# Bf16 products with unread results, placed in four waits of TensorE

## The reference, cut to what matters

```python
h = _L0_tok_ref(x, ...)
h = h + _L0_attn_ref(_layernorm(h, axis=-1), ...)
h = h + _L0_ffn_ref(_layernorm(h, axis=-1), ...)
h = h + _L1_attn_ref(_layernorm(h, axis=-1), ...)
h = h + _L1_ffn_ref(_layernorm(h, axis=-1), ...)

# _L0_tok_ref, for each of 4 layers:
x = _layernorm(x + o, g1[i], be1[i])                      # o: attention output
f = jax.nn.relu(x @ W1[i] + b1[i]) @ W2[i] + b2[i]
x = _layernorm(x + f, g2[i], be2[i])
# then a last _layernorm(x, gf, bf)

# _L0_attn_ref:
qkv = xn @ w_qkv                                          # xn: normalised input
q_l = q.reshape(B, HEADS, M, l, DIM_HEAD).sum(3) / l      # landmarks; k_l likewise
sim1, sim2, sim3 = q @ k_l.T, q_l @ k_l.T, q_l @ k.T      # each through a softmax: a1, a2, a3
left = a1 @ moore_penrose(a2)                             # 6 iterations
out = left @ (a3 @ v) + conv(v)
```

## Time and profile before

| | |
|---|---|
| runs | 1103.89, 1107.82, 1109.42 us; median 1107.82 |
| profiled execution, its own time | 1105.52 us |
| its span | 1103.7 us, 21069 instructions |
| TensorE busy | 974.3 us, 88% |
| VectorE, ScalarE, GpSimd busy | 608.5 (55%), 592.2 (54%), 428.5 us (39%) |
| mean granted clock of TensorE | 0.928 |

### The profile page before, as it was taken

The page is one execution under the profiler, slowest core; times in us unless marked ns, Lnnn a source line. Parts: engine busy times, 40 slices in busy tenths (PEclk is TensorE's granted clock), DMA queues, the critical chain, the costliest instruction groups (busy, mean ns, idle before and its releaser), DMA issues. The chain is left out here.

```text
span 1103.7 us, 21069 instructions
## 1 busy us (share of the span) xinstructions
PE 974.3 (88%) x7350; PEld 711.0 (64%) x7350; DVE 608.5 (55%) x1802; ACT 592.2 (54%) x1332; POOL 428.5 (39%) x630
## 2 busy tenths in 40 slices
PE   2399999999999998626898999996899999997898
PEld 1256676667666665413776776784688888885564
DVE  4366776666667675136353111125377767784773
ACT  4166676676667665326435444316455555543476
POOL 6426777776667766648103000014400010037200
PEclk9699999999999999866698899998799999996899
DMA  4855444555464440010100111100000010006841
GB/s 126 176 106 133 94 94 100 141 117 111 102 154 95 94 94 12 1 33 0 47 3 10 29 30 29 46 8 1 20 10 11 11 56 14 1 1 148 207 97 37
DMA packets 54416, 71.82 MB, mean 65 GB/s; under 512 B 9476, under 2 KB 46624, under 8 KB 50464
## 3 DMA queue, kind: packets, MB, share of 16 engines
q1 hardware_dynamic: 53160, 67.33, 26.2%
q0 software_dynamic: 1152, 3.15, 1.1%
HBM read 48.96 MB, written 17.56 MB: 60 GB/s over the span
## 5 line engine op out<-in xcount | busy, mean ns | idle before, releaser
L2237 DVE TENSOR_REDUCE t_nmax<-banks 128x2 f32<-128x512 f32 x256 | 166.5, 685 | 84.5 <-PE banks L2047 79.3
L2166 ACT ACTIVATE t_probs<-banks 128x512 f32<-128x512 f32 x256 | 144.8, 592 | 79.8 <-PE banks L2069 78.4
L2047 PE MATMUL banks<-t_packed 96*128 96x256 bf16 x512 | 91.2, 278 | 15.3 <-DMA t_packed<-t_qk_pairs 13.3
L2325 POOL TENSOR_SCALAR xhat<-t_rbuf,mv,rstd 128x128 f32<-128x128 f32 x128 | 100.1, 795 | 3.3
L2069 PE MATMUL banks<-t_packed 120*128 120x256 bf16 x512 | 91.5, 276 | 9.3 <-DMA t_packed<-t_mT 8.7
L2047 PEld LDWEIGHTS banks<-t_packed 96*128 96x128 bf16 x512 | 47.5, 99 | 55.0 <-issue 27.0
L863 ACT ACTIVATE hid<-banks,b 128x512 f32<-128x512 f32 x64 | 43.5, 686 | 70.7 <-PE banks L768 70.0
L2069 PEld LDWEIGHTS banks<-t_packed 120*128 120x128 bf16 x512 | 46.3, 98 | 47.5 <-issue 21.0
L1197 ACT ACTIVATE l_probs<-banks,l_shift 128x256 f32<-128x256 f32 x128 | 59.4, 472 | 28.2 <-DVE l_shift L1238 25.5
L906 DVE SCALAR_TENSOR_TENSOR acc<-banks,gates,acc 128x128 f32<-128x128 f32 (+1 forms) x72 | 20.1, 342 | 98.0 <-PE banks L788 98.0
L2082 PE MATMUL banks<-t_probs,t_v 128*32 128x256 f32 x1024 | 72.3, 387 | 0.6 <-ACT t_probs L2166 0.6
(11 more groups left out here) (378 smaller groups left out, 2101.2 us busy)
## 6 DMA issues: line engine op xcount, KB each, us to landing
t_qk_pairs<-t_parts SPq DMA_DIRECT2D x32, 384.0 KB, 2.5
t_packed<-t_qk_pairs SPq DMA_DIRECT2D x32, 384.0 KB, 5.4
t_packed<-t_qk_pairs SPq DMA_DIRECT2D x32, 256.0 KB, 6.0
t_packed<-t_qk_pairs SPq DMA_DIRECT2D x32, 128.0 KB, 6.7
w<-in_L_ffn_w SPq DMA_DIRECT2D x16, 256.0 KB, 2.7
t_packed<-t_mT SPq DMA_DIRECT2D x32, 96.0 KB
g_qk_pairs<-g_parts SPq DMA_DIRECT2D x8, 384.0 KB, 5.3
g_packed<-g_qk_pairs SPq DMA_DIRECT2D x8, 384.0 KB, 4.7
```

The source lines that it names most:

```text
L2047: ins = pe.matmul(m.mbank[:, n % 3, i * S:(i + 1) * S], m.packed[0:MROW, 0, p, h, c + qt * P:c + (qt + 1) * P], m.packed[0:MROW, 1, p, h, ...
L2166: act.activation(m.probs[:, n % 6, :], m.sbank[:, n % 2, :], ACT.Exp).then_inc(sem["probs_ready"], 1)
L2237: dve.tensor_reduce(m.nmax[:, b, u // 4, 2 * hp:2 * hp + 2], m.mbank[:, n % 3, :].rearrange("p (i k) -> p i k", i=2), AX.X, ALU.max, negat ...
L2325: ins = pool.tensor_scalar(m.xhat[:, k, i, :], m.rbuf[:, k, i, :], m.mv[:, k, i, 0:1], m.rstd[:, k, i:i + 1], ALU.subtract, ALU.mult)
```

## The change

A helper issues `count` products of the bf16 identity (128x128) with itself repeated to 512 columns, into a bank that nobody reads at that time. It is called ahead of three items of the mixer, with bank 7, and ahead of C2 of the last pair, with the first bank of `m.mbank`; that one first waits until all maxima are taken. Each call stands ahead of the wait of the item that it precedes.

```diff
--- before.py
+++ after.py
@@ -74,6 +74,12 @@
 MTILES = B + 1
 
 
+def keep_clock(pe, m, bank, count):
+
+    for _ in range(count):
+        pe.matmul(bank, m.identb[:, :], m.identb[:, :].unsqueeze(1).broadcast_to([P, 4, P]), start=True, stop=True)
+
+
 def mixer_order():
 
     order = [("F", 0), ("F", 1), ("F", 2), ("VT",), ("H", 0), ("F", 3), ("VO",), ("H", 1), ("N", 0), ("NT", 0), ("H", 2), ("N", 1),
@@ -94,6 +100,7 @@
     return order
 
 
+CLOCK_PASSES = {("NT", 0): 14, ("NT", 2): 4, ("QK", 2): 5}
 INVERSE = ("SC", "A", "B", "Z")
 
 
@@ -206,6 +213,7 @@
 
             for item in order:
                 kind, g = item[0], item[-1]
+                keep_clock(pe, m, banks[:, 7, :], CLOCK_PASSES.get(item, 0))
                 if kind == "VT":
                     bank = use(("VO",))
                     pe.wait_ge(sem["mix_w_loaded"], 32)
@@ -2111,6 +2119,9 @@
                 filled(step, g, ins)
             elif step in ("C2", "C5"):
                 norm = "C1" if step == "C2" else "C4"
+                if (step, g) == ("C2", LAYER_PAIRS - 1):
+                    pe.wait_ge(sem["max_taken"], 16 * LAYER_PAIRS)
+                    keep_clock(pe, m, m.mbank[:, 0, :], 20)
                 pe.wait_ge(sem["xhat_ready"], apply_at[(norm, g)] + 1)
                 bank = use(step, g)
                 for i in range(4):
```

## The result

The changed kernel takes 1104.18 us (median of 20 runs, 1098.98 to 1110.98), the kernel before 1109.69 us (20 runs, 1103.88 to 1117.08). The ratio is 0.9953, 95% interval [0.9932, 0.9974]: 5.2 us faster, between 2.9 and 7.5.

What follows compares the result with a forecast made beforehand. Bound: a few TensorE waits at the last pair and mixer front, and the half clock behind them. 1.1 + 1.9 = 3.0 us off 1105.52 gives 1102.5; the runs' median lies 2.3 above the profiled execution: 1104.8 us, range 1100.0 to 1109.8.

Steps and rivals of the forecast that it cites:

- Passes at 0.22 us, hidden: Ahead of the last pair's C2: 20 passes at full clock take 4.4 us, inside TensorE's wait of 6.8 us.
- The pair, 1.1 us of 2.2: Last pair, C2's start to C4's: 2.2 us gained if the clock stays full, 0 if not; half taken, 1.1 us.
- The rows on idleness: Trace waits at full clock: 1.7 us passed unharmed; the 2.4 us left at the pair nearer to those losing the clock.
- The front part, 1.9 us: Mixer's front part: passes ahead of NT 0, NT 2 and QK 2 gain 1.9 us, bounds -3 and 2.6.
- QK 3's own 0.9 us: Mixer's front part: QK 3 takes 1.03 us at full clock in place of 1.91 at half, another 0.9 us.
- TensorE as the bound from 517.9 to 541.6: Behind the front part: TensorE, busy 21.9 of 23.7 us at half clock, hands the front part's gain on.
- rival 2: Clock holds on into the stretch of mostly 16-row products from 517.9, saving 3 us more: 1100.0 us; chance 0.08.
- The rule of the Trainium skill on transposes: Transposes don't count as TensorE work for the clock; by it the front part gains nothing and the sum is 1.1 us.
- That the passes don't act on the clock (3): At the pair and NT 0: identity passes, nearly all zeros, leave the clock unchanged, no gain: 1107.8 us; chance 0.12.
- That the nine are met by half clock (5): Passes ahead of NT 2 and QK 2 run at half clock, 3.2 us lost: about 1110.8 us; chance 0.09.
- That the clock holds at both places (1): Clock stays full through last pair and front part, 2.2 + 2.6 = 4.8 us gained: 1103.0 us; chance 0.20.

Runs made afterwards that it cites:

- e5: The changed kernel with no passes at all, only the added wait on max_taken left; ratio to the kernel before 1.0001 [0.9980, 1.0021].
- e1: The changed kernel with only the 20 passes ahead of the last pair's C2, none in the front part; ratio to the kernel before 0.9964 [0.9934, 0.9995].
- e4: The changed kernel with only the 4 passes ahead of NT 2 and 5 ahead of QK 2; ratio to the kernel before 1.0017 [0.9993, 1.0042].
- e3: The kernel before plus the wait and 31 passes ahead of the last pair's C2, none in the front part; ratio to the kernel before 0.9955 [0.9924, 0.9985].
- e2: The changed kernel with only the front part's 14, 4 and 5 passes, none at the pair; ratio to the kernel before 0.9957 [0.9933, 0.9982].
- e7: The changed kernel with 31 passes at the pair, not 20, and 24 more between the 16-row products; ratio to the kernel before 0.9954 [0.9931, 0.9977].
- e9: The changed kernel measured again without an edit, in a second group of runs; ratio to the kernel before 0.9955 [0.9927, 0.9983].
- e6: The changed kernel with 31 passes in place of 20 ahead of the last pair's C2; ratio to the kernel before 0.9951 [0.9923, 0.9979].

## Why the prediction was right, point by point

**The time.** Forecast 1104.8 us; measured 1104.18, in the range. The gain forecast was 3.0 us and the measured one 5.2 [2.9, 7.5]. That the two times agree within 0.6 us is luck: the kernel before came out at 1109.69 in 20 runs, not 1107.82 as in three, 1.9 us higher, and the gain was forecast 2.2 us too small. The two nearly cancel.

**Passes at 0.22 us, hidden.** Right. Twenty took 4.48 us (0.22 each), the four and five at full clock 1.04 and 1.25. All 31 fit into the wait. The added wait costs nothing (e5).

**The pair, 1.1 us of 2.2.** The mechanism was right and so was the bound (6.25 us; 6.3 had been read off the pair before). The term of the sum was too large by the profiled executions: the pair took 8.46 us on the mean of three with 20 passes and 8.90 on the mean of five without (8.51, 8.76, 8.84, 9.16, 9.25), 0.45 us, and since the two sets overlap even that is not clear of their scatter. One of the three is the slowest execution of e1, so the mean over all executions may be more; it is not known. The rows on idleness had said that 2.4 us is among the lengths that lose the clock, and half the gain was taken nevertheless. A fall that comes later puts C2 at full clock but keeps C3 at half longer (e1).

**The front part, 1.9 us.** Right in its steps as far as QK 3. NT 0 was not late, the hand-overs went as ScalarE's steps said (N 2 1.94 us earlier, forecast 2.0), and q 2 waited 0.24 us (0.3). QK 3's own 0.9 us was a property of the execution shown: four other executions without the 14 passes had it at 1.03. From NT 0's start to QK 3's end it is 14.25 us in five executions with all three groups of passes against 15.74 on the mean of five without the 14, 1.5 us.

Behind QK 3 the step that failed is what hands the gain on. The prediction had TensorE as the bound from 517.9 to 541.6, with nothing gained there. But in the same trace TensorE waits in that stretch for VectorE's a2 (1.35 us, to 528.75), and a2 of the second pair stands beside GpSimd's memsets:

```profile
522.40 1.80 POOL L602 MEMSET inv<- 128x2048 f32 x1
522.70 1.94 DVE L528 TENSOR_SCALAR mx_a<-mx_e,mx_sums 128x64 f32<-128x64 f32 x1
```

With the 14 passes a2 comes before them (the rows at e4). From QK 3's end to the pseudo-inverse it is then 12.84 us on the mean of the same five against 14.13, another 1.3 us that the sum did not have. The whole front is 27.1 us (27.76, 27.67, 27.35, 26.29, 26.36) against 29.87 (29.81 to 30.08): 2.8 us. A clock that stays full into the 16-row products also has a part (26.3 where it lasted to about 17.5 us behind NT 0, 27.4 to 27.8 where it fell after 15.2 to 15.5), a small piece of rival 2; in e4 it had none. How the 1.3 us divide between the two was not tested. The clock never lasted through the stretch.

**Transposes.** NT 0 to NT 3 did not let the clock fall; 1.00 from 504.9 to 521.8. The rule of the Trainium skill on transposes that the forecast weighed (TensorE: Matmul & The Clock Gate, Part 4: PE-mode transpose) was taken to mean that the front part gains nothing; that did not come. It is no proof against the rule: the four groups of transposes are 2.6 of the 12.4 us that TensorE is busy there, and the rest is other products.

**The rivals.** That the passes don't act on the clock (3) fell with e3, and with the clock's rise among the 14 passes in all eight executions that have them. That the nine are met by half clock (5) was not seen; e4's 1.0017 is its nearest trace. (By its own terms, 1107.8 + 3.2, its time should read 1111.0, not 1110.8.) That the clock holds at both places (1) is what 26 or 31 passes do.

**What stays open.** The stretches give 0.45 + 2.8 = 3.2 us, inside the measured interval but below its middle. The clearest gap is e1: its three lengths lie among those of the executions without passes, and its ratio is 0.9964 with 1 outside the interval. There the profiled execution, the slowest of twelve, may be at fault. For the changed kernel one candidate for the rest is the inverse, in which the clock fell once in some executions and not in others. Two tables of stretches show it, e5 with the fall (554.2 to 557.4) and e2 without it, where the mean of 0.92 comes from the half clock up to 541.7 alone:

```profile
554.20:557.40 3.20, 3.20 (x51) 2.75 (x46) 0.98 (x4) 0.80 (x3) 0.00 (x0) 0.50 0.03 5
557.60:587.00 29.40, 25.53 (x474) 21.89 (x472) 16.82 (x71) 10.82 (x38) 1.46 (x3) 1.00 0.01 3
```

```profile
533.70:581.00 47.30, 41.54 (x636) 35.74 (x636) 23.26 (x91) 19.75 (x80) 6.51 (x12) 0.92 0.02 5
```

The inverse is 47.5 to 48.2 us without that fall and 49.4 to 50.4 with it. The seven executions with passes at NT 0 and NT 2 had it twice (e7, e9), the other six five times (before was the one without). The inverse is 1.5 us shorter on the mean of the seven, but with 13 executions it may be chance, and nothing here shows why the passes should act so far behind. Whether 31 passes at the pair are better than 20 was not resolved either by the ratios (0.9951 to 0.9958 against 0.9953 and 0.9955); by the pair's own length they are 2.2 us better in the profiled executions.

## What to carry to other kernels

Passes with unread results help where TensorE idles in a wait, loses the clock, and then stands alone on the chain that sets the end; fill such a wait until what stays idle is short, because a partly filled one only puts the fall off, into the work that was to be sped up. Where TensorE has no wait to hide them in, passes have to win back their own time: in e7's profiled execution 24 of them lengthened the front by 4.7 us, and its twelve runs showed no gain over e6. Look at what the other engines do where the gain is to be handed on: here almost half of the front's gain appeared behind QK 3, where VectorE got ahead of GpSimd's memsets. When the parts of a change are each worth less than a run's scatter, measure lengths between two steps inside each profiled execution, several executions of each kind, and check by the clocks and times of all runs whether the profiled one is typical.

## What the runs showed that was not expected

The same code takes different times in its unchanged parts: C1 of the last pair started between 456.1 and 462.5 us in the 13 profiled executions, the pair without passes took 8.51 to 9.25 us, the inverse 47.5 to 48.2 or 49.4 to 50.4. In each the half-clock stretches lie at other places relative to the work: QK 3 was at 1.91 us in one execution without the 14 passes and at 1.03 in the four others. VO's end to NT 0, a chain without TensorE, took 5.79 or 5.80 us in every one.
